# Blocks of nodes taken fullest and emptiest in turn, in a three-layer graph attention kernel

## The reference

```python
# layers 1 and 2 (H = 8), after h = relu(norm(x)) @ w_in + b_in; every node also has an edge to itself
xn = layernorm(h); q, k, v = xn @ wq + bq, xn @ wk + bk, xn @ wv + bv
scores = (q[dst] * k[src]).sum(-1) / sqrt(DH)
attn = exp(scores - segment_max(scores, dst)[dst]); attn = attn / segment_sum(attn, dst)[dst]
h = h + segment_sum(attn * v[src], dst) @ wo + bo
h = h + gelu(layernorm(h) @ w1 + b1) @ w2 + b2
# layer 3 (H = 4), on relu(norm(x)): the key of an edge gets 0.2 * rel_w[edge type] added, no feed-forward part
out = norm(agg @ Wo + bo + h) * gamma + beta;  x = x + out
```

## Time and profile before

| | |
|---|---|
| median of 3 runs | 4808.43 us (4798.98 to 4812.11) |
| profiled execution, first to last instruction | 4807.7 us |
| mean granted clock of TensorE | 0.832 |
| busy: PE / DVE / POOL / ACT | 76% / 74% / 64% / 39% of the span |
| first gather of layer 1, 2, 3 | 578.6, 1943.2, 3307.7 us |

### The profile page before, as it was taken

One profiled execution on the slowest core, in us unless ns is written; L12 is line 12 of the kernel. 1 busy time (PEld: TensorE's weight loads), 2 busy tenths in 40 slices (PEclk: granted clock), 3 DMA queues, 4 the chain that ended last, 5 costly groups with the idle time before them and its releaser, 6 DMA issues. The chain is left out here.

```text
span 4807.7 us, 99510 instructions
## 1 busy us (share of the span) xinstructions
PE 3632.4 (76%) x17128; PEld 2684.6 (56%) x17129; DVE 3571.0 (74%) x5452; ACT 1888.0 (39%) x4155; POOL 3097.6 (64%) x2969
## 2 busy tenths in 40 slices
PE   8875448888899999278888999995656666666666
PEld 6432136666666676256666777774445555544544
DVE  7732167777788885577888888874799888888866
ACT  3442113343444455033434454553333333334343
POOL 0053167777777773577777777763677777777653
PEclk9887678999999999688999999997777677766766
DMA  3362556776677673577766776653556555555442
GB/s 124 152 177 84 126 162 198 225 215 210 209 229 218 206 223 115 157 213 218 221 209 204 239 231 219 216 180 101 161 178 193 178 169 177 174 168 161 143 142 70
DMA packets 384185, 864.67 MB, mean 180 GB/s; under 512 B 160913, under 2 KB 173671, under 8 KB 384118
## 3 DMA queue, kind: packets, MB, share of 16 engines
q0 software_dynamic: 232080, 680.08, 47.6%
q1 hardware_dynamic: 151720, 183.05, 11.4%
q10 hardware_dynamic: 318, 0.84, 0.0%
HBM read 791.89 MB, written 143.30 MB: 195 GB/s over the span
## 5 line engine op out<-in xcount | busy, mean ns | idle before, releaser
L1249 POOL DMA_INDIRECT kv<-kv_dram,idx x2616 | 2736.1, 1046 | 974.5 <-issue 727.6
L1801 PE MATMUL ps_acc<-kv,ident 128*128 x5232 | 1341.9, 421 | 55.0 <-DVE kv L1418 41.8
L1801 PEld LDWEIGHTS ps_acc<-kv,ident 128*128 128x128 f32 x5232 | 1108.0, 215 | 317.4 <-issue 140.5
L1313 DVE TENSOR_TENSOR kv<-kv,ps_q 128x1024 f32 x654 | 786.7, 1215 | 268.7 <-DMA kv<-kv_dram,idx 234.4
L1318 DVE TENSOR_REDUCE sc<-kv 128x32 f32 (+2 forms) x654 | 784.5, 1211 | 15.5 <-DVE kv L1313 13.1
L1418 DVE TENSOR_TENSOR kv<-kv,ps_q x654 | 753.6, 1216 | 3.5 <-DVE sm L1542 3.2
L1629 ACT COPY agg<-ps_acc 128x256 f32<-128x256 f32 x147 | 54.8, 372 | 1438.4 <-issue 737.4
L1795 PE MATMUL ps_acc<-acc_scaled,ident 128*128 128x256 f32 x306 | 146.7, 575 | 429.5 <-DVE acc_scaled L1382 429.5
L1852 PE MATMUL ps_big<-xnaT,w_ffn 128*128 128x128 f32 x3136 | 374.1, 278 | 2.8 <-ACT xnaT L1692 2.8
L1852 PEld LDWEIGHTS ps_big<-xnaT,w_ffn 128*128 128x128 f32 x3136 | 357.9, 192 | 14.6 <-issue 3.3
L1865 PE MATMUL ps_w<-w_ffn,shared 128*128 128x256 f32 x1568 | 364.6, 386 | 0.0
(11 more groups left out here) (215 smaller groups left out, 4817.4 us busy)
## 6 DMA issues: line engine op xcount, KB each, us to landing
rec_dram<-rec_out SPq DMA_DIRECT2D x98, 512.0 KB, 4.4
rec_in<-rec_dram SPq DMA_DIRECT2D x98, 512.0 KB, 4.9
kv<-kv_dram,idx POOLq DMA_INDIRECT x2616, 3.7
rec_by_node<-rec_in SPq DMA_DIRECT2D x49, 512.0 KB
windows<-kv SPq DMA_DIRECT2D x49, 384.0 KB
kv_dram<-rec_in SPq DMA_DIRECT2D x49, 256.0 KB
rec_out<-in_x SPq DMA_DIRECT2D x48, 128.0 KB
w_ffn<-in_L_gnn_w SPq DMA_DIRECT2D x4, 1024.0 KB, 6.4
```

The costliest lines, as they stand in the source:

```text
L1249: pool.indirect_dma_start(kv[:, u * W + slot, :], None, kv_dram[l], bass.IndirectOffsetOnAxis(ap=idx[:, u, slot:slot + 1], axis=0), bounds ...
L1313: nc.vector.tensor_tensor(at, at, q, ALU.mult).then_inc(s["mul"], 1)
L1801: mm = nc.tensor.matmul(ps_acc[:, 0:D], ident[:], at[:, :, slot, :].rearrange("p a d -> p (a d)"), start=False, stop=False, skip_group_che ...
```

## The change

After the rank `r` of every node is summed up, six DVE operations on 128 x 49 numbers move it. `total` becomes the block `q = r // 128` (the rank less 63.5, divided by 128, rounded to the nearest whole number by adding and subtracting 12582912). `total_in` is `97 - 3q`, and `rank` becomes `r + 128 * min(q, 97 - 3q)`: block `q` is now block `min(2q, 97 - 2q)`, with the same partition. The old block 0 stays at 0, old 48 comes at 1, old 1 at 2, old 47 at 3, and so on to old 25 at 47 and old 24 at 48. In chunks: 8, 2, 7, 3, then five times (6, 3), two times (5, 3), thirteen times (5, 4), and 4, 4, 4, 4, 4. The contents of each block, the number of rounds and of chunks are the same.

```diff
                 def ranks():
                     step(nc.vector.tensor_reduce(rank_f, before.rearrange("p (c b) -> p b c", b=NB), AX_X, ALU.add))
+                    step(nc.vector.tensor_scalar(total, rank_f, 1.0 / P, -(P - 1) / (2.0 * P), ALU.mult, ALU.add))
+                    step(nc.vector.tensor_scalar(total, total, 12582912.0, None, ALU.add))
+                    step(nc.vector.tensor_scalar(total, total, 12582912.0, None, ALU.subtract))
+                    step(nc.vector.tensor_scalar(total_in, total, -3.0, float(2 * NB - 1), ALU.mult, ALU.add))
+                    step(nc.vector.tensor_tensor(total, total, total_in, ALU.min))
+                    step(nc.vector.scalar_tensor_tensor(out=rank_f, in0=total, scalar=float(P), in1=rank_f,
+                                                        op0=ALU.mult, op1=ALU.add))
                     nc.vector.tensor_copy(payload[:, :, 1], first)
```

## The result

The changed kernel takes **4838.99 us** (median of 4 runs, 4834.33 to 4839.27) against 4807.45 (4 runs, 4798.98 to 4812.11): a ratio of 1.0066, 95% interval 1.0054 to 1.0078. It is slower by 0.66%, 31.5 us. The forecast was 4786, its range ended at 4822, and the sign is wrong. The profiled execution took 4834.33 us with a span of 4832.6, so it stands 4.7 us under its median.

The account below looks back on a forecast made before the run. No engine was busy throughout: POOL's gathers bound larger blocks and PE 3-blocks in layers 1 and 2, the relation chain layer 3's 4- and 3-blocks. -12 - 13 + 3 + 0 = -22 us took 4807.7 to 4786; range 4752 to 4822.

Parts of the forecast that it names:

- the prediction's own signs of being wrong: POOL waiting for DVE before 6-blocks, (5, 4) pairs over 52.2 us in layers 1 and 2, layer 3 moving over 10 us.
- Layer 1, -12 forecast: Layer 1: up to 18 us gained from POOL's pauses and PE's late tail, less 6 lost in pairs: -12 us.
- some 3 us, hidden in the pauses that the two-round blocks make anyway: Layer 1, after the 2-block at place 1: POOL waits some 3 us for DVE, at no cost.
- the 15 us lost in the pairs: Layer 1: (6, 3) and (5, 3) pairs exceed POOL's need by 10 + 5 us; 9 recovered, loss 6.
- Layer 2, -13 forecast: Layer 2: 3 us more to win than layer 1 in its 3-blocks, 2 given back for slower fixed program: -13 us.
- Layer 3, +3 forecast: Layer 3: pairs bound by the relation chain or DVE's loop give +4.5, -2.4 and -6.5, ends +7: +3 us.
- 33.8 a block, of which 3 x 1.15 fall away: Layer 3, DVE's loop: a 6-block takes 33.8 us, after a 3-block only 30.3, as fewer chunks are weighed.
- The ends: Layer 3: the 2-block at place 1 pays the chain and a 4-block comes last: +7 us together.
- The stage ahead: Before the layers: six more DVE operations, 0 to 7 us, hidden in POOL's 39.9 us idle time: cost 0.
- Rival 1: Layers 1 and 2: pairs lose their whole 15 us, tails gain only 9 each; total 4802 us; chance 33%.
- Rival 2: Averaging works fully: POOL never waits in layers 1 and 2, layer 3 gains 17 us; total 4752; chance 8%.
- Rival 3: Layer 3: relation chain with sums at the lower clock costs +38 us; total 4821, slower; chance 16%.

Follow-up runs that it names:

- f1: Changed kernel plus one more POOL drain per layer, after the second of the last five scatters: 4813.17 us, ratio 1.0015 to the kernel before.
- f2: Kernel before plus one more POOL drain per layer, after the second of the last five scatters: 4800.53 us, ratio 0.9989 to the kernel before.
- f4: Changed kernel with the 2-chunk block put last and the further POOL drain in each layer: 4796.43 us, ratio 0.998 to the kernel before.
- g1: Kernel before, reordered with each 3-block between 5-blocks, plus the early POOL drain: 4770.27 us, ratio 0.9924 where the kernel before took 4805.0.

## Why the prediction was wrong, step by step

Forecast -22 us, measured +24.9 in the profiled executions, 47 apart: 21.6 the DRAINs, 16.6 the rest of layer 3, 6.4 and 2.2 the rest of layers 1 and 2. Of the prediction's own signs of being wrong one came, layer 3 moved by over 10 us; POOL didn't wait for DVE ahead of the 6-blocks, and the (5, 4) pairs kept to 52.25.

**The end of a layer: the term was missing, 21.6 us.** The sum followed POOL to its last gather and PE to its last sums and took the drain of the pipeline behind them as unchanged. It holds an instruction whose length depends on the order of POOL's DMAs, 2.3 us in one order and 9.3 in another. "What the profile will show" had no row for it. f1 shows it by removal: 25.8 us between the medians.

**Layer 1, -12 forecast; -5.6 measured without the DRAIN (+1.4 less 7.0), of it 1.7 the clock at PE's last matmuls.** f1 against f2 has -2.9. The time from the last gather to the last sums shrank by 7.9 of the 9 us (29.0 to 21.1). POOL's part was to gain 3 (9 back, 6 lost) and lost 3: from the first to the last gather it takes 1286.2 us, 1283.1 before. f1 runs the same order and takes 1289.4, so single us of this are within what two runs differ by. Two places:

```profile
644.32 1.00 POOL L1256 DMA_INDIRECT kv<-kv_dram,idx  x1 [6.73 <-PE ps_acc L1808]
...
709.58 0.99 POOL L1256 DMA_INDIRECT kv<-kv_dram,idx  x1 [1.59 <-ACTq L1630]
...
1018.51 1.03 POOL L1220 DMA_INDIRECT kv_dram<-rec_out,scatter_to  x1 [2.18 <-issue]
...
1022.24 1.02 POOL L1256 DMA_INDIRECT kv<-kv_dram,idx  x1 [2.70 <-PE ps_acc L1808]
...
1071.09 1.02 POOL L1256 DMA_INDIRECT kv<-kv_dram,idx  x1 [1.95 <-PE ps_acc L1808]
```

The third block of six or more begins at 709.6 where it began at 673.4: 36.2 later. The 2- and the 3-block ahead of it need 29.2 of that (12.0 + 17.2; no scatter is issued yet for the first five blocks, which saves 1.3 each). The other 7.0 are POOL's wait, 6.4 of them after the 2-block, until PE had summed. This wait had been put at "some 3 us, hidden in the pauses that the two-round blocks make anyway". It was twice that and wasn't hidden. And in the two (5, 3) pairs POOL lost 4.2 and 1.9 us: from weighing to weighing they take 49.2 us (49.9 forecast) against POOL's 47, and the lead was by then at its limit. The profile names PE's sums as what ended 2.7 and 1.95 us of these pauses; the pause of 2.2 us ahead of the scatter has no releaser.

Of the 15 us lost in the pairs 9 were to be recovered. The (6, 3) pairs gave no loss at POOL at all (52.3, its need), the (5, 3) pairs 6.1. So the net 6 came out, but not by its parts, and that is partly luck: at DVE the (6, 3) pairs take 52.9 us and not 54.3. The forecast's "five more chunks at 2.3", 11.5 us from a 6-block's first product to its last, are 10.2 in the trace (786.02 to 796.19).

**Layer 2, -13 forecast, -10.8 without the DRAIN** (-3.8 less 7.0), of it 1.5 the clock at PE's last matmuls; f1 against f2 has -9.8. Right within 2 to 4 us.

**Layer 3, +3 forecast; +27.2, of it 7.6 the DRAIN and 19.6 the order** (19.3 from f1 against f2). From the first to the last scaling of a block's own row on DVE the layer takes 1450.0 us against 1435.9. The pairs were to give -4.4 and gave +8: (6, 3) came to 62.2 (61.8 forecast), (5, 3) to 57.4 (56.5), (5, 4) to 58.05 (57.4). PE in a (5, 4) pair, from the start of a 4-block's sums over a 5-block's to the next 4-block's start:

```profile
4315.73 1.22 PE L1802 MATMUL ps_acc<-acc_scaled,ident 128*128 128x256 f32 x2 [4.24 <-DVE acc_scaled L1389]
...
4326.55 0.18 PE L1811 MATMUL ps_acc<-zeros_b,ident_b 128*128 128x32 bf16 x1
...
4344.52 1.22 PE L1802 MATMUL ps_acc<-acc_scaled,ident 128*128 128x256 f32 x2 [4.88 <-DVE acc_scaled L1389]
...
4356.35 0.18 PE L1811 MATMUL ps_acc<-zeros_b,ident_b 128*128 128x32 bf16 x1
...
4373.79 1.22 PE L1802 MATMUL ps_acc<-acc_scaled,ident 128*128 128x256 f32 x2 [4.24 <-DVE acc_scaled L1389]
```

The 4-block starts 29.27 us after the 5-block's start: 11.8 of sums and 17.4, the forecast's 11.7 + 17.7 = 29.4. The 5-block starts 28.8 after the 4-block, not 28.0. The step that failed is DVE's loop: "33.8 a block, of which 3 x 1.15 fall away". 33.8 is the mean over a window of the earlier trace rows that holds five steps from one block's weighing to the next: 33.7, 33.5, 35.4, 35.5, and 30.7 for the first 5-block. The last two steps from a 6-block to a 6-block are the 35.4 and 35.5. From these the same rule gives 32.0 for 6 after 3, where the forecast had 30.3 and 31.6 were measured. The 3 after the 6 took 30.6 and not 31.5, which hides most of it in the pair's sum. For 5 after 4 the rule gives 29.4 from the 30.6 of 5 after 5, less 1.15; the 28.8 measured lie between that and the 28.0. Thirteen pairs at 0.65 us, five at 0.4 and two at 0.9 are the 12 us.

The ends were estimated at +7 and came to about 11: the 2-block at place 1 takes 25.6 us where it took 18.2 last, and the last block's sums take 11.1 in place of 7.0. f4 removes both and gains 11.0 in the layer.

**The stage ahead, 0.** 578.7 against 578.6. That it agrees to 0.1 us is luck: over the runs on such chips the first gather comes at 574.1 to 581.7 us. No cost of the six operations is seen in that.

**The rivals.** Rival 1 asked for tails that gain and pairs that give back all of their 15 us; they gave back 6. Rival 2 is out: POOL did wait in layer 1, and layer 3 without its DRAIN is 19.6 us longer, not 17 shorter. Rival 3 forecast slower by 13 us through sums at the lower clock, from 0.9 us a pair on; its pairs cost 0.4 more than before (8 over 20), the 5-blocks' sums took 11.8 and not 12.8, the granted clock of the (5, 4) pairs is 0.74 where the 5-blocks had 0.70 and the 4-blocks 0.69. Rival 3 had the side right for the wrong reason. The Trainium skill's sentence (TensorE: Matmul & The Clock Gate, Part 1), that activity releases the throttle, doesn't contradict this, but no run separates it.

## What to carry to other kernels

Balance along a pipeline has to be reckoned with the chain between neighbours, in both directions: what the small one waits for after the large one, and the reverse. A group wins only if these add up to less than what the bounding engine needs for the group. Sums of busy time said (4, 3) would win 12 to 14 us a layer, and it lost 5 in layer 1 and nothing in layer 2; the chain said (5, 5, 3) would win 11 and it won 15, in layer 1. And read the instructions between the last useful work and the barrier before calling a reordering free there.

## What was not expected of the hardware

- POOL's DRAIN takes 82 ns for each indirect DMA issued since some point, 0.29 us after three and 8.24 after a hundred. The gathers themselves aren't slowed by what piles up: they follow each other at 1.3 us throughout.
- From where it counts is open. Of the 970 DMAs in each of layers 1 and 2 and the 921 of layer 3 the DRAIN's length counts 14 to 113, by the order; counted back from the layer's end, the count begins in each of the twelve cases at most two DMAs behind the start of a block. The same sequence gives the same length, whatever the chip: the first stage's DRAIN takes 8.24 us in every run, and the early DRAINs of g1 took 5.55, 5.54 and 3.86 us (within 0.01) on all three of its chips. A drain at a place where POOL idles leaves the closing one only the few that follow.
- A DRAIN of PE spans the matmuls that are still to run: ten of them took 3.56 us at a granted clock of 1.00 and 5.0 to 5.3 at 0.66 to 0.68, at the same place of the program. Why the clock was lower there in one run and not in another is open.
- Two chips took 6660 to 6780 us where others take 4805, with the granted clock at 0.74 in place of 0.83 and unexplained pauses before single matmuls. The cause stays open.
